# Layer 0 of a graph network stack on one core: two tiles a visit in place of three

## The chip, the core and the metric

The kernel runs on one core of a Trainium2 chip, in one launch. TensorE (PE in the profile) multiplies matrices into the eight banks of PSUM, VectorE (DVE), ScalarE (ACT) and GpSimd (POOL) work on vectors, and SP (SyncE) issues transfers. Each runs its own program in order, and they wait for one another through counting semaphores. The metric is the time of one execution in microseconds on the device.

## What is computed

Four layers over 2048 nodes with 64 features, each `x = x + layer(relu(layernorm(x)), adj)`. The change is in layer 0 alone, an attention with 8 heads and two kinds of edges (adj is 0 or 1):

```python
Q = h @ Qw + Qb; K = h @ Kw + Kb; V = h @ Vw + Vb
S1 = einsum('id,kdh->ikh', Q, A1); S2 = einsum('jd,kdh->jkh', K, A2)
e = S1[rows[:, None], kidx] + S2[rows[None, :], kidx]
e = leaky_relu(e, negative_slope=0.2)
attn = softmax(e, axis=1)
out = einsum('ijh,jhd->ihd', attn, Vh).reshape(n, h * d) @ Pw + Pb
```

The scores are rank-one sums, so exp(leaky_relu(s1 + s2)) can be built from products and maxima of exponentials of vectors, which is what the kernel does, with no exponential per element.

## The kernel before

**Tiles.** A tile is one head, 128 source nodes j and 512 target nodes i. There are 8 heads x 4 blocks of i x 16 tiles of j = 512 tiles (TILES0), numbered k, with j fastest. 16 tiles in a row share a block of i: a row block.

**One tile's way through the engines.** GpSimd writes the value for edges of kind 0 into one of 16 ring buffers in SBUF (line 368). TensorE crosses two vectors, held as three bf16 parts each, into the PSUM slot k mod 6 (`cross`, line 1053, 18 rows deep; in the profile "18*128"). ScalarE applies ReLU with scale -1 in place (line 851). TensorE adds a second product onto it, the floor (`raise_floor`, line 1061, "9*128"). VectorE copies the slot into the ring buffer where adj is 1 (`select`, copy_predicated, line 530). The finished tile is then read twice by TensorE: by `aggregate` (line 1074, fp32, two tiles at once, each in 64 columns of the array, into bank 6) and by `denominators` (line 1084, fp32, four tiles at once, each in 32 columns, into bank 7). An aggregate is 4 matmul records in the trace, a denominator 8. Per four tiles there are two aggregates and one denominator; one of these three is a "unit", and there are 384 units.

Tile k uses the 32 rows of the array from 32 (k mod 4) on, for its cross and its floor.

**The order on TensorE.** It is written out by hand as visits v. A visit issues the floors of the tiles that visit v - 1 crossed (`trio(v - 1)`), then the crosses of `trio(v)`, then the units from `units(v)` to `units(v + 1)`. The first unit comes in visit 3. A floor waits for its ReLU (`relus`), a cross for the select of the tile six before it, whose slot it takes (`selected`), an aggregate for the selects of its two tiles.

**The others.** ScalarE goes over the same visits: the ReLUs of `trio(v)`, and with the tenth and eleventh unit of every twelve the copies of bank 6 (line 839, `main_out`) and bank 7 (line 846, `den_out`) out of PSUM, at the end of a row block. VectorE selects tile by tile, with a small reciprocal (lines 537 and 538) and an addition (line 546) once per row block. GpSimd fills the ring in the order of the tiles and waits for a denominator before it writes over four old tiles; once per row block it also normalises (line 356). SP moves the denominators out and back and stages the next heads' vectors.

Of the kernel before, what the change touches and what calls it, by code (L numbers as in the profile page):

```python
# [42 lines left out]
def gnn_stack(nc, x_d, adj_d, Qw, Qb, Kw, Kb, Vw, Vb, a_rel, Pw, Pb, w_k, w_q, W2, a2, out_d):  # L43
# [14 lines left out]
    BLOCKS = N // HALF  # L58
    PER_HEAD = BLOCKS * NT
    SLOTS = 6  # L60
    TRIO = 3
    MAIN, DEN = 6, 7
    BLKS = 4
    NINE = PARTS * PARTS
# [4 lines left out]
    with ctx:  # L69
# [141 lines left out]
        BY_ROW = H * BLOCKS - 2  # L211
        VISITS = -(-TILES0 // TRIO)
        UNITS = TILES0 // 4 * 3

        def units(v):

            return min(max(9 * (v - 3) // 4, 0), UNITS)

        def trio(v):

            return range(TRIO * v, min(TRIO * v + TRIO, TILES0)) if 0 <= v < VISITS else ()

        LAST = next(v for v in range(2 * VISITS) if units(v) == UNITS)

        block = ctx.enter_context(nc.Block())
# [566 lines left out]
        def _(act):  # L792
# [55 lines left out]
            for v in range(LAST):  # L848
                for k in trio(v):
                    act.wait_ge(s["crossed"], k + 1)  # L850
                    act.activation(ps[:, k % SLOTS, :], ps[:, k % SLOTS, :], ACT.Relu, scale=-1.0).then_inc(s["relus"], 1)  # L851
                for u in range(units(v), units(v + 1)):
                    if u % 12 == 10:
                        main_out(u // 12)
                    if u % 12 == 11:
                        den_out(u // 12)
# [77 lines left out]
        def _(pe):  # L934
# [157 lines left out]
            for v in range(LAST):  # L1092
                for k in trio(v - 1):
                    raise_floor(k)
                for k in trio(v):
                    cross(k)
                for u in range(units(v), units(v + 1)):
                    if u % 3 < 2:
                        aggregate(4 * (u // 3) + 2 * (u % 3))
                    else:  # L1100
                        denominators(4 * (u // 3))
# [201 lines left out]
```

## Time and profile before

| | us |
|---|---|
| median of 3 runs | 1080.58 |
| lowest, highest | 1079.04, 1087.63 |
| the profiled execution | 1082.16 |
| its span | 1079.9 |
| layer 0's loop in it, first cross to last denominator | 92 to 574 |

| engine | busy us, share of the span |
|---|---|
| TensorE matmuls | 937.5, 87% |
| VectorE | 728.5, 67% |
| GpSimd | 555.8, 51% |
| ScalarE | 546.0, 51% |

The granted clock of TensorE is 0.888 of full in the mean over the span. The span is from the first to the last instruction that the profiler saw. In the timelines one row is a run of equal instructions: start and length in us, engine, line, operation, what it writes and reads with shapes, count, and in brackets how long the engine was idle before and what ended that. The length of a run reaches to the end of its last instruction, so runs of a pipelined engine overlap.

### The profile page before, as it was taken

How to read it: one execution, taken by the hardware profiler on the slowest of the kernel's cores; microseconds unless marked ns; L12 is line 12 of the kernel's file. 1: busy time of each engine (PE TensorE's matmuls, PEld its weight loads, DVE VectorE, ACT ScalarE, POOL GpSimd, SP SyncE). 2: the span in 40 equal slices, each digit the busy share in tenths (PEclk: the TensorE clock that was granted, in tenths of full speed). 3: DMA queues.
4: the chain of work that ended last, by engine and by line, in shares of the span. 5: the costliest groups of instructions: out<-in, count | busy, mean ns of one | idle time of the engine just before them, and what ended most of it. 6: DMA issues, size and time to landing. Idle time of an engine off the chain costs nothing.

```text
span 1079.9 us, 14479 instructions
## 1 busy us (share of the span) xinstructions
PE 937.5 (87%) x5239; PEld 336.0 (31%) x5239; DVE 728.5 (67%) x1145; ACT 546.0 (51%) x943; POOL 555.8 (51%) x658
## 2 busy tenths in 40 slices
PE   1996999999999999999996599999667939999970
PEld 1762222222222222222223522333262334555430
DVE  3145777777778777777774567411328667999987
ACT  0374666666665666656660076100100137899970
POOL 2006788898889888888870000000000007799962
PEclk8566999999999999999997579999857965999995
DMA  9472002021211121120000000000000000000000
GB/s 196 64 156 80 12 21 75 21 71 33 66 38 59 33 67 35 28 73 22 22 21 1 0 1 1 1 1 1 1 0 39 1 1 0 1 1 1 1 0 19
DMA packets 24940, 34.05 MB, mean 32 GB/s; under 512 B 16219, under 2 KB 16363, under 8 KB 23718
## 3 DMA queue, kind: packets, MB, share of 16 engines
q1 hardware_dynamic: 22566, 24.75, 7.9%
q0 software_dynamic: 2304, 8.39, 4.4%
q8 instruction: 41, 0.67, 0.3%
q14 instruction: 29, 0.24, 0.1%
HBM read 40.22 MB, written 1.30 MB: 38 GB/s over the span
## 4 chain that ended last, share of the span: by engine, by line
PE 72%; DVE 16%; issue 4%; DMA 3%; SPq 2%; ACT 1%; POOL 1%; DVEq 0%; ACTq 0%; POOLq 0%
PE ps L1074 22%; PE ps L1084 11%; PE ps L1181 8%; PE ps L1061 5%; DVE big L411 4%; PE ps L1053 4%; PE ps L1215 3%; PE ps L1155 3%; PE ps L1251 3%; DVE big L724 2%; DMA big<-in_L_gnn_Pw_dram 2%; DVE big L408 2%; PE ps L1145 2%; PE ps L938 1%; PE ps L1223 1%
## 5 line engine op out<-in xcount | busy, mean ns | idle before, releaser
L530 DVE COPY_PREDICATED big<-mask,ps 128x512 f32<-128x512 uint8 x512 | 338.2, 724 | 115.2 <-PE ps L1061 107.6
L368 POOL TENSOR_SCALAR big<-big 128x512 f32<-128x512 f32 x512 | 356.3, 713 | 72.5 <-PE ps L1084 72.2
L851 ACT ACTIVATE ps<-ps 128x512 f32<-128x512 f32 x512 | 266.8, 582 | 167.1 <-PE ps L1053 167.1
L1074 PE MATMUL ps<-big 128*64 128x512 f32 x1024 | 258.9, 613 | 0.0
L380 POOL TENSOR_TENSOR big<-big 128x512 f32<-128x512 f32 x40 | 67.3, 1684 | 342.1 <-ACT big L911 342.1
L1084 PE MATMUL ps<-big 128*32 128x512 f32 x1024 | 136.5, 605 | 0.0
L1053 PE MATMUL ps<-op_r,op_l 18*128 18x512 bf16 x512 | 110.3, 386 | 8.4 <-DMA op_r<-split_scratch 7.1
L1074 PEld LDWEIGHTS ps<-big 128*64 128x64 f32 x1024 | 58.6, 136 | 135.7 <-issue 98.4
L1251 PE MATMUL ps<-big 66*128 66x512 f32 x160 | 86.1, 668 | 2.2 <-DVE big L697 1.3
L411 DVE TENSOR_TENSOR big<-big,mask 128x512 f32<-128x512 f32 (+1 forms) x72 | 65.8, 933 | 12.8 <-ACT big L871 11.5
L1061 PE MATMUL ps<-op_r,op_l 9*128 9x512 bf16 x512 | 70.7, 390 | 2.0 <-ACT ps L851 2.0
L384 POOL TENSOR_TENSOR big<-big 128x512 f32<-128x512 f32 x40 | 63.6, 1590 | 6.7 <-ACT big L919 2.0
L617 DVE TENSOR_REDUCE work<-ps 128x256 f32<-128x512 f32 x16 | 11.1, 691 | 77.9 <-PE ps L1165 77.9
L1061 PEld LDWEIGHTS ps<-op_r,op_l 9*128 9x128 bf16 x512 | 17.2, 91 | 145.3 <-ACT ps L851 106.0
L1181 PE MATMUL ps<-big,y_nat 128*64 128x512 f32 x256 | 59.0, 609 | 1.9 <-DVE y_nat L407 1.9
L879 ACT ACTIVATE hT<-ps 128x512 f32<-128x512 f32 x16 | 9.2, 598 | 92.3 <-PE ps L1181 89.0
L938 PE MATMUL ps<-ident,h_nat 128*65 128x128 f32 (+1 forms) x64 | 13.9, 407 | 41.9 <-DVE h_nat L411 18.1
L1084 PEld LDWEIGHTS ps<-big 128*32 128x32 f32 x1024 | 20.1, 107 | 83.3 <-issue 83.3
L1267 PE MATMUL ps<-big,h_nat 128*66 128x512 f32 x80 | 43.0, 625 | 2.8 <-DVE big L411 2.8
L1251 PEld LDWEIGHTS ps<-big 66*128 66x128 f32 x160 | 30.9, 210 | 38.2 <-issue 18.2
L667 DVE SCALAR_TENSOR_TENSOR big<-big,mask 128x1024 f32<-128x1024 f32 x32 | 38.4, 1280 | 4.9 <-DMA big<-max_scratch 4.9
L871 ACT ACTIVATE big<-ps,small 128x1024 f32<-128x1024 f32 x32 | 34.0, 1111 | 13.4 <-PE ps L1145 13.2
(235 smaller groups left out, 1137.1 us busy)
## 6 DMA issues: line engine op xcount, KB each, us to landing
big<-max_scratch SPq DMA_DIRECT2D x9, 1024.0 KB, 4.9
big<-in_adj_dram POOLq DMA_DIRECT2D x16, 512.0 KB, 6.5
big<-rden_scratch SPq DMA_DIRECT2D x30, 256.0 KB, 3.3
op_l<-split_scratch SPq DMA_DIRECT2D x64, 36.0 KB
op_r<-split_scratch SPq DMA_DIRECT2D x64, 36.0 KB
x_nat<-in_x_dram SPq DMA_DIRECT2D x1, 512.0 KB, 4.1
out_dram<-x_nat SPq DMA_DIRECT2D x1, 512.0 KB, 3.8
den_scratch<-y_nat SPq DMA_DIRECT2D x30, 8.0 KB
```

The source lines that it names most:

```text
L368: pool.tensor_scalar(ring[:, k % RING, :], vrow[:, head % 2, i0:i0 + HALF], HUGE, g0[:, head, jt:jt + 1], ALU.min, ALU.max).then_inc(s["ba ...
L380: pool.tensor_tensor(wB[:, u, :], wB[:, u, :], wA[:, u, :], ALU.subtract).then_inc(s["ratio"], 1)
L384: pool.tensor_tensor(wD[:, u, :], wD[:, u, :], wC[:, u, :], ALU.subtract).then_inc(s["art"], 1)
L411: return dve.tensor_tensor(out, a, b, op)
L530: dve.copy_predicated(ring[:, k % RING, :], mask[:, jt, i0:i0 + HALF], ps[:, k % SLOTS, :])\
L851: act.activation(ps[:, k % SLOTS, :], ps[:, k % SLOTS, :], ACT.Relu, scale=-1.0).then_inc(s["relus"], 1)
L1053: pe.matmul(ps[:, k % SLOTS, :], op_l[g:g + 2 * NINE, head % 2, jt * P:(jt + 1) * P], op_r[g:g + 2 * NINE, head % 2, i0:i0 + HALF], start= ...
L1061: pe.matmul(ps[:, k % SLOTS, :], op_l[g:g + NINE, head % 2, jt * P:(jt + 1) * P], op_r[g:g + NINE, head % 2, i0:i0 + HALF], start=False, s ...
L1074: m = pe.matmul(ps[w * D:(w + 1) * D, MAIN, :], vp[:, head, jt + w, :], ring[:, (u + w) % RING, :], start=(jt == 0), stop=(jt == NT - 2))
L1084: m = pe.matmul(ps[32 * w:32 * (w + 1), DEN, :], q0[:, head, jt + w:jt + w + 1].to_broadcast([P, 32]), ring[:, (u + w) % RING, :], start=( ...
L1181: m = pe.matmul(ps[w * D:(w + 1) * D, 4 + c, :], Y[n - 1][:, jt, :], eT[:, jt, c * HALF:(c + 1) * HALF], start=(jp == 0), stop=(jp == NT / ...
L1251: pe.matmul(ps[:, bank, :], lhs3[0:DX, jt * P:(jt + 1) * P], rhs[0:DX, c * HALF:(c + 1) * HALF], start=True, stop=True).then_inc(sem, 1)
```

## The change

Two numbers of layer 0's order: a visit holds two tiles instead of three, and the units advance by 3/2 a visit instead of 9/4. Per tile that is 3/4 of a unit either way. The six PSUM slots stay as they are.

```diff
@@ -58,7 +58,7 @@
     SLOTS = 6
-    TRIO = 3
+    TRIO = 2
     MAIN, DEN = 6, 7
@@ -214,7 +214,7 @@
         def units(v):
 
-            return min(max(9 * (v - 3) // 4, 0), UNITS)
+            return min(max(3 * (v - 3) // 2, 0), UNITS)
```

TensorE's program at the start of the loop before (L1053 cross, L1061 floor, L1074 aggregate with two instructions of the program each, L1084 denominator with four):

```order
L1053 MATMUL ps<-op_r,op_l 128x512 x3
L1074 MATMUL ps<-big 64x512 x4
L1061 MATMUL ps<-op_r,op_l 128x512 x3
L1053 MATMUL ps<-op_r,op_l 128x512 x3
L1084 MATMUL ps<-big 32x512 x4
L1074 MATMUL ps<-big 64x512 x2
L1061 MATMUL ps<-op_r,op_l 128x512 x3
L1053 MATMUL ps<-op_r,op_l 128x512 x3
L1074 MATMUL ps<-big 64x512 x2
L1084 MATMUL ps<-big 32x512 x4
```

and the same place of the changed program:

```order
L1053 MATMUL ps<-op_r,op_l 128x512 x2
L1074 MATMUL ps<-big 64x512 x2
L1061 MATMUL ps<-op_r,op_l 128x512 x2
L1053 MATMUL ps<-op_r,op_l 128x512 x2
L1074 MATMUL ps<-big 64x512 x2
L1084 MATMUL ps<-big 32x512 x4
L1061 MATMUL ps<-op_r,op_l 128x512 x2
L1053 MATMUL ps<-op_r,op_l 128x512 x2
L1074 MATMUL ps<-big 64x512 x2
L1061 MATMUL ps<-op_r,op_l 128x512 x2
```

Between the crosses and the next floors there were always two or three units; now there is one aggregate, or an aggregate and a denominator, by turns, to the end of the loop.

ScalarE's program where row blocks end (L851 the ReLU, L839 and L846 the two copies), before:

```order
L839 ACTIVATE big<-ps 128x512
L851 ACTIVATE ps<-ps 128x512 x3
L846 ACTIVATE y_nat<-ps 128x512
L851 ACTIVATE ps<-ps 128x512 x15
L839 ACTIVATE big<-ps 128x512
L846 ACTIVATE y_nat<-ps 128x512
```

and in the changed program:

```order
L851 ACTIVATE ps<-ps 128x512 x16
L839 ACTIVATE big<-ps 128x512
L846 ACTIVATE y_nat<-ps 128x512
L851 ACTIVATE ps<-ps 128x512 x16
L839 ACTIVATE big<-ps 128x512
L846 ACTIVATE y_nat<-ps 128x512
```

The two copies now always follow the ReLUs of one and the same visit, where before ReLUs of a visit stood between them in one row block of three.

## Rows read from the trace of the kernel before

**Rows 1.** The page: busy shares, the chain by engine and line, costly groups.

```profile
PE 937.5 (87%) x5239; PEld 336.0 (31%) x5239; DVE 728.5 (67%) x1145; ACT 546.0 (51%) x943; POOL 555.8 (51%) x658
...
PE 72%; DVE 16%; issue 4%; DMA 3%; SPq 2%; ACT 1%; POOL 1%; DVEq 0%; ACTq 0%; POOLq 0%
PE ps L1074 22%; PE ps L1084 11%; PE ps L1181 8%; PE ps L1061 5%; DVE big L411 4%; PE ps L1053 4%; PE ps L1215 3%; PE ps L1155 3%; PE ps L1251 3%; DVE big L724 2%; DMA big<-in_L_gnn_Pw_dram 2%; DVE big L408 2%; PE ps L1145 2%; PE ps L938 1%; PE ps L1223 1%
...
L530 DVE COPY_PREDICATED big<-mask,ps 128x512 f32<-128x512 uint8 x512 | 338.2, 724 | 115.2 <-PE ps L1061 107.6
L368 POOL TENSOR_SCALAR big<-big 128x512 f32<-128x512 f32 x512 | 356.3, 713 | 72.5 <-PE ps L1084 72.2
```

**Rows 2.** Busy time by engine in one stretch, visits 5 to 171.

```profile
core 0: us, PE busy (x) PEld busy (x) DVE busy (x) ACT busy (x) POOL busy (x), PEclk, DMA share, GB/s
106.42:568.16 461.74, 460.43 (x2993) 100.31 (x2992) 356.81 (x585) 290.90 (x559) 392.57 (x531) 1.00 0.14 41
```

**Rows 3.** The chain that ended last, by time: start us, us, engine, line.

```profile
216.53 0.32 PE ps L1061 x3
216.85 0.21 PE ps L1053 x3
217.07 1.01 PE ps L1074 x4
218.07 0.99 PE ps L1084 x8
...
223.01 1.87 PE ps L1074 x8
...
227.42 0.32 PE ps L1061 x3
227.74 0.57 PE ps L1053 x3
```

**Rows 4.** Waits, weight loads only, 106 to 568 us: total us, times, longest.

```profile
PEld ps L1053 <- DVE big L530: 12.4, 32, 1.1
```

**Rows 5.** Timeline of TensorE, 224.80 to 224.90 us: start, us, line, tiles.

```profile
224.81 0.39 PE L1061 MATMUL ps<-op_r,op_l 9*128 9x512 bf16 x3
224.82 0.39 PE L1053 MATMUL ps<-op_r,op_l 18*128 18x512 bf16 x1
```

**Rows 6.** Timeline of all engines, the loop's last two visits with floors.

```profile
564.77 0.59 PE L1053 MATMUL ps<-op_r,op_l 18*128 18x512 bf16 x2
...
565.29 1.07 ACT L851 ACTIVATE ps<-ps 128x512 f32<-128x512 f32 x2 [0.98 <-PE ps L1053]
...
568.16 0.39 PE L1061 MATMUL ps<-op_r,op_l 9*128 9x512 bf16 x2
...
568.48 1.94 PE L1074 MATMUL ps<-big 128*64 128x512 f32 x8
```

**Rows 7.** Timeline of all engines, the loop's start: start, us, idle before.

```profile
97.45 1.56 ACT L851 ACTIVATE ps<-ps 128x512 f32<-128x512 f32 x3 [0.73 <-PE ps L1053]
...
98.08 1.58 PE L1061 MATMUL ps<-op_r,op_l 9*128 9x512 bf16 x3 [0.70 <-ACT ps L851]
...
99.07 0.61 PE L1053 MATMUL ps<-op_r,op_l 18*128 18x512 bf16 x3
...
99.61 3.68 PE L1074 MATMUL ps<-big 128*64 128x512 f32 x8
...
103.22 0.61 PE L1061 MATMUL ps<-op_r,op_l 9*128 9x512 bf16 x3
```

**Rows 8.** Timeline of all engines where a row block ends.

```profile
131.01 0.59 PE L1053 MATMUL ps<-op_r,op_l 18*128 18x512 bf16 x3
131.14 0.60 ACT L846 ACTIVATE y_nat<-ps 128x512 f32<-128x512 f32 x1
...
131.63 1.57 ACT L851 ACTIVATE ps<-ps 128x512 f32<-128x512 f32 x3
```

**Rows 9.** Busy time by engine in one stretch of layer 2, columns as rows 2.

```profile
821.00:869.00 48.00, 44.01 (x282) 14.99 (x278) 37.36 (x36) 5.93 (x10) 0.00 (x0) 0.99 0.00 1
```

## The prediction

> **What bounds the kernel now.** I read the page first. TensorE is busy 87% of the span and carries 72% of the chain that ended last; lines 1074 and 1084, the aggregates and denominators of layer 0, are the largest pieces of it [rows 1]. So I asked for the layer 0 loop alone, cut from the floors of visit 5 (106.42 us) to those of visit 171 (568.16 us). That is 166 visits of three tiles, 498 tiles in 461.74 us at full granted clock, 0.927 us a tile, and TensorE shows 460.43 us busy while VectorE shows 356.81, ScalarE 290.90, GpSimd 392.57 [rows 2]. The change touches only this loop, and every tile that gets dearer by 10 ns costs 5 us.
>
> A busy share of 99.7% does not say that nobody waits: a matmul's time in the trace covers its pipeline, so short stalls vanish in it. The chain of work in order of time is better. One pattern of four visits (12 tiles) runs from 216.53 to 227.42 us, 10.89 us, and its pieces are: floors of three tiles 0.32 us, then crosses 0.21, an aggregate alone 1.01, a denominator 0.99, two aggregates in a row 1.87 [rows 3]. Sum: 4 x 0.53 + 2 x 1.87 + 2 x 1.01 + 3 x 0.99 = 10.85. At that pace 498 tiles need 41.5 x 10.89 = 452 us; the missing 10 us are visits in which a cross stands for its slot, as the last piece shows (0.57 in place of 0.21) [rows 3]. The view of waits has them under line 1053 waiting for VectorE's select, 32 times [rows 4]. These waits are what two tiles a visit on six slots can remove.
>
> **The change, part by part.**
>
> *Matmuls.* Nothing is added or removed: 512 crosses, 512 floors, 256 aggregates, 128 denominators either way. Only the grouping moves. Per 12 tiles there were four visits; now there are six, alternately "floors 2, crosses 2, one aggregate" and "floors 2, crosses 2, one aggregate, one denominator".
>
> *Floors with crosses.* Tile k uses row strip 32 (k mod 4). With three tiles, the floors take three strips and only the first cross finds the fourth strip free: it starts 0.01 us after the floors, together with them [rows 5], and the other two wait for a strip, which is the 0.21 piece in the chain [rows 3]. With two tiles the floors and crosses of one visit are four tiles in a row, so four different strips, and all four can run together. Four at once is what rows 5 already show. The price is then that of one batch: in the last visit before, two floors with no cross behind them, the aggregate starts 568.48 - 568.16 = 0.32 us after the floors [rows 6]. So 6 x 0.32 = 1.92 replaces 4 x 0.53 = 2.12. From the other side, if the crosses did not join, it is 0.53 per visit (a rival below).
>
> *Aggregates.* No two aggregates stand in a row any more. Two pairs of 1.87 become four of 1.01: +0.30 per 12 tiles [rows 3]. TensorE's own work is then 1.92 + 6 x 1.01 + 3 x 0.99 = 10.95 per 12 tiles, against 10.85 of before by the same pieces: even, to 0.1 us. The Trainium skill, page "TensorEngine Tiling", Key Properties, says that a change of tiling mode drains TensorE, which speaks against smaller groups: here the runs of one kind rise from 11 to 15 per 12 tiles. The chain's pieces already hold that price (a lone aggregate is 0.07 dearer than half a pair), so the rule adds nothing to the sum.
>
> *Slots.* The second cross of visit v waits for the select of tile 2v - 5, whose floor was issued at the start of visit v - 2, so two whole visits (3.96 us together, below) lie between; before, it was the visit just ahead (2.4 to 3.4 us) for three selects of 0.72 us plus the odd row addition. I take the 10 us of waits as gone.
>
> *The ReLU between cross and floor.* This is the part that costs. TensorE runs in order, and visit v + 1 opens with the floors of the tiles that visit v crossed; each needs its ScalarE pass. In full-clock rows: from the crosses to the first ReLU 565.29 - 564.77 = 0.52 us; two ReLUs together 1.07 us [rows 6]; from the end of the last ReLU to the floor and the crosses behind it 99.07 - (97.45 + 1.56) = 0.06 at most, take 0.05 [rows 7]. Cross to second floor is 0.52 + 1.07 + 0.05 = 1.64 us and cannot be shorter. What covers it before: two or three units, so 0.53 + 1.87 = 2.40 at the least, against 0.52 + 1.56 + 0.05 = 2.13 for three ReLUs; hidden, with 0.27 to spare. After: a visit with an aggregate and a denominator is 0.32 + 1.01 + 0.99 = 2.32, hidden. A visit with one aggregate is 0.32 + 1.01 = 1.33, and the second floor is ready only at 1.64. TensorE stands 0.31 us, with the next two crosses queued behind that floor, and ScalarE starts its next two ReLUs later in turn, so nothing catches up. A visit got 1/3 shorter in TensorE's work, but the chain cross-ReLU-floor lost only one ReLU of 0.49.
>
> The Trainium skill, page "ScalarE: Activation LUTs", Rules for kernel authors, budgets about 0.3 us and 0.83 ns an element for an ACTIVATE, so 0.72 us for these by estimate; two would be 1.45, the one-aggregate visit 2.02, and the loss some 47 us larger. The trace does not agree: two in a row take 1.07 [rows 6], and the row decides.
>
> *Row blocks.* Once in 16 tiles ScalarE also copies the main and the denominator bank. In an existing visit of just the new kind (one aggregate, one denominator) the denominator's copy starts at 131.14 and the next ReLU at 131.63, where the cross at 131.01 alone would allow 131.53 [rows 8]: 0.10 us late. Before it was inside the 0.27 of slack. After, the visit that follows is a one-aggregate visit, where lateness counts: 31 x 0.10 = 3.1 us.
>
> *Other engines.* GpSimd fills ring slots released by denominators (0.71 us a tile) and VectorE selects at 0.72 [rows 1]; four tiles now take 3.96 us, more than either's 2.9, so both have more room. SP's row staging follows the blocks and gets more time too.
>
> *Start and end.* Visits 0 to 2 hold no unit, and each is shorter by one ReLU, -1.5 us; but more of the first units then fall before the clock rises (a pair of aggregates takes 3.61 us there, from 99.61 to 103.22, against 1.87 [rows 7]), which takes back some 0.7. After the last floors one unit fewer is left, with its share of waiting: -0.5. Together about -1.3.
>
> **Sum.** Four tiles: 1.64 + 2.32 = 3.96. 498 tiles: 124.5 x 3.96 = 493.0, + 3.1 = 496.1, against 461.7: +34.4. With start and end: +33. The profiled execution took 1082.2 us (span 1079.9), so 1115; the median of the timed runs is 1.6 lower, 1080.6, so I forecast 1114.
>
> **Rivals.**
> 1. *The ReLU is hidden after all, not slower* (7%). Then four tiles take TensorE's own 1.33 + 2.32 = 3.65, 498 tiles 454, the waits of the crosses are gone, and the kernel takes 1082 - 7 - 1 = 1074, for the timed median 1072. It needs the second floor to be ready 1.33 us after its cross: ReLU latency and work smaller by 0.31 of 1.64, that is the 0.52 of rows 6 nearly halved or the two ReLUs at 0.38 each. For it: rival 1 is what a count of busy time says, since ScalarE is busy only 63% of the loop. Against it: all three terms are rows, and they repeat at the start, where floors do follow ReLUs directly [rows 7].
> 2. *The crosses do not join the floors* (4%). Each visit then opens with 0.53; the cross comes 0.21 behind the second floor, so 1.85 + 2.53 = 4.38, 498 tiles 545 + 3, and the kernel takes 1168. For it: two crosses behind two floors are in no row. Against it: rows 5, with four strips at work.
> 3. *The clock falls in the gaps* (3%). TensorE would now stand 0.31 of 3.96 us, 8%. In a stretch of layer 2 with 3.99 us idle of 48 (8%) the granted clock read 0.99 [rows 9], that is the 2.4 GHz level nearly throughout. If a tenth of the loop fell to 1.2 GHz, where aggregates take 3.61 in place of 1.87, it would cost about 0.1 x 0.93 x 454 = 42 us more: 1156. The Trainium skill, page "TensorE: Matmul & The Clock Gate", A second HAM failure mode, describes a kernel whose clock oscillated on short idles between groups while it cycled PSUM; this row shows hardly any at the same idle share.
>
> **How the numbers follow.** Forecast mechanism 86%, rivals 7, 4, 3. A measurement of this kernel tells about 1% from no change, 10.8 us. The chain term is 1.64 with 0.03 either way (+-4 us), the 10 us of cross waits might remain in part (up to +5), and half of the block term might not show (-2); a partly hidden ReLU wait of 0.25 in place of 0.31 would give 1107. Range 1105 to 1126. Rival 1 lies at -0.8%, mostly "same": faster 0.03, same 0.05, slower 0.92.
>
> **What would show it.** Per four tiles, floor to floor: 1.64 and 2.32, by turns. Crosses starting within 0.02 us of the floors ahead of them, and the aggregate 0.32 after. In the waits, line 1061 idle behind line 851 in about 128 visits, as at the start, and line 1053 behind VectorE gone. ScalarE busy the same, about 291 us over a loop of 496. It is wrong if the one-aggregate visits last 1.33 (rival 1) or the aggregate comes 0.53 after the floors (rival 2), or the granted clock in 110 to 600 us is below 1.00 (rival 3).

## The result, and the profile after

The changed kernel takes 1113.7 us in the median of four runs (1110.5 to 1118.7), the kernel before 1079.8 beside it: a ratio of 1.0305, 95% interval 1.0236 to 1.0374. It is slower by 34 us. The profiled execution took 1111.3 us with a span of 1109.1.

| | before | after |
|---|---|---|
| up to layer 0's first cross | 92.3 us | 95.2 us |
| layer 0 loop, first cross to last denominator's start | 481.4 us | 516.5 us |
| four tiles, mean over the 498 tiles from tile 12 on | 3.71 us | 3.98 us |
| from there to the end | 506.2 us | 497.4 us |
| span | 1079.9 us | 1109.1 us |

The page of the kernel after, in the order of [rows 1]: busy shares, the chain by engine and line, and VectorE's select.

```profile
PE 967.6 (87%) x5239; PEld 337.8 (30%) x5239; DVE 740.4 (67%) x1145; ACT 553.3 (50%) x943; POOL 556.1 (50%) x658
...
PE 76%; DVE 15%; issue 4%; DMA 2%; ACT 2%; SPq 1%; DVEq 0%
PE ps L1074 23%; PE ps L1084 11%; PE ps L1061 11%; PE ps L1181 7%; DVE big L411 4%; PE ps L1215 3%; PE ps L1155 3%; PE ps L1251 2%; PE ps L1004 2%; PE ps L965 2%; DVE big L724 2%; DMA big<-in_L_gnn_Pw_dram 2%; DVE big L408 2%; PE ps L938 1%; PE ps L1145 1%
...
L530 DVE COPY_PREDICATED big<-mask,ps 128x512 f32<-128x512 uint8 x512 | 343.8, 726 | 135.0 <-PE ps L1061 132.8
```

The share of line 1061, the floors, in the chain doubled, from 5 to 11%, with as many floors as before. The select costs the same per instruction, 0.73 us, and VectorE only waits longer for the floors. The loop in the columns of [rows 2], cut from a pair of visits near its start to one near its end:

```profile
109.50:606.00 496.50, 495.00 (x2994) 105.23 (x2992) 367.39 (x584) 297.95 (x561) 391.57 (x529) 1.00 0.13 38
```

TensorE reads 99.7% busy again, at full clock again, in a stretch in which it stands 0.28 us of every 3.94. The busy share shows nothing of it. The chain in order of time does (start, length, what; compare [rows 3]):

```profile
202.61 0.32 PE ps L1061 x2
202.94 0.01 PE ps L1053 x2
202.94 1.01 PE ps L1074 x4
203.95 0.60 PE ps L1061 x2
204.55 0.01 PE ps L1053 x2
204.56 1.01 PE ps L1074 x4
205.56 0.99 PE ps L1084 x8
206.56 0.32 PE ps L1061 x2
```

The floors of one visit take 0.32 us and those of the next 0.60, by turns, and the crosses 0.01: they run with the floors, where before they added 0.21. From 202.61 to 206.56 is 3.95 us for four tiles. The same place in the timeline of all engines, whose starts are up to 0.07 us earlier than the chain's, says why the second pair of floors takes 0.60:

```profile
202.55 0.39 PE L1061 MATMUL ps<-op_r,op_l 9*128 9x512 bf16 x2
...
202.55 0.39 PE L1053 MATMUL ps<-op_r,op_l 18*128 18x512 bf16 x2
...
202.87 1.08 PE L1074 MATMUL ps<-big 128*64 128x512 f32 x4
203.04 1.07 ACT L851 ACTIVATE ps<-ps 128x512 f32<-128x512 f32 x2 [1.29 <-PE ps L1053]
...
203.88 0.67 PE L1061 MATMUL ps<-op_r,op_l 9*128 9x512 bf16 x2
204.16 0.09 PEld L1061 LDWEIGHTS ps<-op_r,op_l 9*128 9x128 bf16 x1 [0.19 <-ACT ps L851]
...
204.17 0.39 PE L1053 MATMUL ps<-op_r,op_l 18*128 18x512 bf16 x2
```

In this one-aggregate visit the crosses start at 202.55 together with the floors, the aggregate 0.32 us later at 202.87, the two ReLUs at 203.04. The next visit opens with its first floor at 203.88 as soon as the aggregate leaves room, second floor at 204.16 when the second ReLU (203.04 + 1.07 = 204.11) is done, crosses right behind. 204.16 - 202.55 = 1.61 us. The weight load of the second floor is idle until then, put down to ScalarE. In the waits between 100 and 600 us:

```profile
PEld ps L1061 <- ACT ps L851: 234.6, 373, 1.6
...
PEld ps L1053 <- DVE big L530: 0.6, 1, 0.6
```

The first row holds much idle time of weight loads that lies beside running matmuls, so its sum is no loss; the second is: one late cross in place of the 32 of [rows 4].

After the loop the changed kernel is 8.8 us quicker, in code that the change doesn't touch. The same columns, the rest of the program, after and then before:

```profile
612.20:1109.00 496.80, 386.96 (x1759) 179.64 (x1755) 331.69 (x489) 209.73 (x323) 138.02 (x83) 0.85 0.01 4
```

```profile
574.30:1079.90 505.60, 398.03 (x1755) 186.10 (x1755) 331.25 (x489) 209.94 (x323) 137.95 (x83) 0.83 0.01 4
```

The last column but two is the granted clock: 0.85 against 0.83. VectorE's busy time agrees within 0.5 us; TensorE's is 11 us less. Which stretches of the later layers run at 1.2 and which at 2.4 GHz differs between these two executions, and I put the 8.8 us down to it; no run varies it alone. The start of the loop is touched as well: up to the floor of tile 12 the kernel before took 14.2 us from its first cross here and 13.6 in the run e9_before_short_add below, with the same code up to there. From tile 12 on the loop runs at 1.00, so the experiments below are read by their loop and periods as well as by their time.

### The profile page after: what moved, and what is told of

It is laid out like the page before. It is cut to its first block, busy times and chain, and to the rows that moved or that the text cites. A ratio compares the mean times of both kernels' runs of the same rounds, so it can differ in the third digit from the quotient of the medians.

```text
span 1109.1 us, 14479 instructions
## 1 busy us (share of the span) xinstructions
PE 967.6 (87%) x5239; PEld 337.8 (30%) x5239; DVE 740.4 (67%) x1145; ACT 553.3 (50%) x943; POOL 556.1 (50%) x658
## 4 chain that ended last, share of the span: by engine, by line
PE 76%; DVE 15%; issue 4%; DMA 2%; ACT 2%; SPq 1%; DVEq 0%
PE ps L1074 23%; PE ps L1084 11%; PE ps L1061 11%; PE ps L1181 7%; DVE big L411 4%; PE ps L1215 3%; PE ps L1155 3%; PE ps L1251 2%; PE ps L1004 2%; PE ps L965 2%; DVE big L724 2%; DMA big<-in_L_gnn_Pw_dram 2%; DVE big L408 2%; PE ps L938 1%; PE ps L1145 1%
## 5 line engine op out<-in xcount | busy, mean ns | idle before, releaser
L530 DVE COPY_PREDICATED big<-mask,ps 128x512 f32<-128x512 uint8 x512 | 343.8, 726 | 135.0 <-PE ps L1061 132.8
L851 ACT ACTIVATE ps<-ps 128x512 f32<-128x512 f32 x512 | 274.4, 579 | 193.1 <-PE ps L1053 193.1
L1074 PE MATMUL ps<-big 128*64 128x512 f32 x1024 | 277.7, 621 | 0.0
L1061 PE MATMUL ps<-op_r,op_l 9*128 9x512 bf16 x512 | 139.3, 388 | 3.2 <-ACT ps L851 2.0
L1084 PE MATMUL ps<-big 128*32 128x512 f32 x1024 | 136.8, 606 | 0.0
L1061 PEld LDWEIGHTS ps<-op_r,op_l 9*128 9x128 bf16 x512 | 35.2, 90 | 242.8 <-ACT ps L851 241.4
L1053 PE MATMUL ps<-op_r,op_l 18*128 18x512 bf16 x512 | 100.8, 389 | 1.5 <-DVE mask L522 1.2
L1251 PE MATMUL ps<-big 66*128 66x512 f32 x160 | 81.4, 631 | 4.4 <-DVE big L724 2.2
L1074 PEld LDWEIGHTS ps<-big 128*64 128x64 f32 x1024 | 50.9, 135 | 59.4 <-issue 32.5
L1084 PEld LDWEIGHTS ps<-big 128*32 128x32 f32 x1024 | 20.1, 107 | 104.7 <-issue 104.7
L1251 PEld LDWEIGHTS ps<-big 66*128 66x128 f32 x160 | 28.5, 199 | 38.1 <-issue 15.2
## 6 DMA issues: line engine op xcount, KB each, us to landing
big<-in_adj_dram POOLq DMA_DIRECT2D x16, 512.0 KB, 8.3
x_nat<-in_x_dram SPq DMA_DIRECT2D x1, 512.0 KB, 4.2
out_dram<-x_nat SPq DMA_DIRECT2D x1, 512.0 KB, 3.8
```

Of the source, the lines that this page charges most:

```text
L530: dve.copy_predicated(ring[:, k % RING, :], mask[:, jt, i0:i0 + HALF], ps[:, k % SLOTS, :])\
L1053: pe.matmul(ps[:, k % SLOTS, :], op_l[g:g + 2 * NINE, head % 2, jt * P:(jt + 1) * P], op_r[g:g + 2 * NINE, head % 2, i0:i0 + HALF], start= ...
L1061: pe.matmul(ps[:, k % SLOTS, :], op_l[g:g + NINE, head % 2, jt * P:(jt + 1) * P], op_r[g:g + NINE, head % 2, i0:i0 + HALF], start=False, s ...
L1074: m = pe.matmul(ps[w * D:(w + 1) * D, MAIN, :], vp[:, head, jt + w, :], ring[:, (u + w) % RING, :], start=(jt == 0), stop=(jt == NT - 2))
L1084: m = pe.matmul(ps[32 * w:32 * (w + 1), DEN, :], q0[:, head, jt + w:jt + w + 1].to_broadcast([P, 32]), ring[:, (u + w) % RING, :], start=( ...
L1251: pe.matmul(ps[:, bank, :], lhs3[0:DX, jt * P:(jt + 1) * P], rhs[0:DX, c * HALF:(c + 1) * HALF], start=True, stop=True).then_inc(sem, 1)
```

## The experiments

All edits are to the changed kernel unless said. "Loop" is from the first cross to the last denominator's start in the profiled execution, and a period is the time from a floor to the floor four tiles later.

### Is it the ReLU? Half of each ReLU

```diff
-act.activation(ps[:, k % SLOTS, :], ps[:, k % SLOTS, :], ACT.Relu, scale=-1.0)
+act.activation(ps[:, k % SLOTS, 0:HALF // 2], ps[:, k % SLOTS, 0:HALF // 2], ACT.Relu, scale=-1.0)
```

> The changed kernel with the ReLU on 256 of each slot's 512 columns (the other half of the scores goes without it). Theory (TensorE waits for the second ReLU in each one-aggregate visit): cross to second floor falls from 1.61 to about 1.2 us, under the 1.33 us that the aggregate covers, so a pair of visits takes 1.34 + 2.33 = 3.67 us in place of 3.94, the 0.15 us at each row block goes too: -35 - 4, so 1073 to 1077 us. Rival (the loss is TensorE's own, in changing more often between kinds of matmul): nothing moves, 1113.

> The kernel before with the same cut, ReLU on half of each slot's columns. Theory: in its visits the ReLU has 0.27 us to spare, so nothing is gained, 1080 within 0.5%. Rival (ScalarE's work sets the pace in either kernel): 10 us or more are gained.

Measured: 1073.8 us (10 runs) for the changed kernel with the cut, loop 475.3 against 516.5; ratio to the kernel before 0.997 (0.992 to 1.002). For the kernel before with the cut 1080.7 us, ratio 1.002 (0.997 to 1.006), loop 479.1 against 481.4. The timeline of the cut changed kernel in a one-aggregate visit right behind a row block: crosses, the copy of bank 7, the two ReLUs, the next floors:

```profile
200.14 0.39 PE L1053 MATMUL ps<-op_r,op_l 18*128 18x512 bf16 x2
200.27 0.60 ACT L846 ACTIVATE y_nat<-ps 128x512 f32<-128x512 f32 x1 [0.42 <-PE ps L1084]
...
200.76 0.65 ACT L851 ACTIVATE ps<-ps 128x256 f32<-128x256 f32 x2
...
201.47 0.39 PE L1061 MATMUL ps<-op_r,op_l 9*128 9x512 bf16 x2
```

Even this one, with the ReLUs held back by the copy until 200.76, is over at 201.47, 1.33 us after its crosses, both floors at once. The period is 3.67 us everywhere but in one place, at a row block too. So the loss hangs on the length of the ReLU chain. With the ReLUs short in both kernels the finer cutting is no loss: the changed one's loop is the shorter by 3.8 us (475.3 against 479.1), since the joined crosses and the missing late ones outweigh what single aggregates cost. In the kernel before, where two or three units cover three ReLUs, the cut is worth 2.3 us of loop and nothing measurable in the whole. This also gives the price of the rival that I had put at 7%: it would have come out at 1072 to 1074.

### Do the crosses join because their strips are free?

```diff
-g = 32 * (k % 4)
+g = 32 * (k % 2)
```

in `cross` and `raise_floor`.

> The changed kernel with tile k on row strip 32 (k mod 2), so that two crosses find both strips taken by two floors. Theory (the crosses join the floors only because their strips are free): the crosses start 0.21 us after the floors; a pair takes 2.54 + 1.82 = 4.36 us in place of 3.94, 128 pairs: +54, 1167 us. Rival (the strips don't matter; the crosses are short anyway): within 10 us of 1114.

Measured: 1159.8 us, ratio 1.078 (1.066 to 1.089), period 4.305, loop 564.2. The chain:

```profile
303.62 0.32 PE ps L1061 x2
303.95 0.22 PE ps L1053 x2
304.16 1.01 PE ps L1074 x4
305.17 0.54 PE ps L1061 x2
305.71 0.22 PE ps L1053 x2
```

The crosses cost 0.22 again in every visit. It came 7 us under what was expected: I had priced a one-aggregate visit at 1.82 us, and it is 1.77. The strips' worth is (4.305 - 3.944) x 128 = 46 us: without four strips the change would have cost 80 us in place of 34.

### Were the late crosses of before worth 10 us, and did the slots' slack remove them?

```diff
-SLOTS = 6
+SLOTS = 4
```

> The changed kernel with four PSUM slots in place of six: a cross waits for a select whose floor came one visit before, not two. Theory (six slots at two tiles a visit took the cross waits away): the second cross after a one-aggregate visit waits until some 1.9 us after the floors, +0.28 us a pair and more where VectorE has a row block's extra work, 1145 to 1160 us, and line 1053 stands behind VectorE over 100 times. Rival (the slack in slots is worth nothing): 1114.

Measured: 1176.8 us, ratio 1.093 (1.083 to 1.104), loop 576.6. Slower than either expectation. Periods are 4.21; from tile 108 on, where VectorE's first row addition stands, one of four is 5.11. The chain where a row block's addition stands, and, from 304.96 on, an ordinary pair:

```profile
301.19 0.61 PE ps L1061 x2
301.80 0.73 DVE big L530
...
302.57 0.39 PE ps L1053
...
304.96 0.32 PE ps L1061 x2
305.28 0.01 PE ps L1053 x2
305.29 1.01 PE ps L1074 x4
306.30 0.60 PE ps L1061 x2
306.89 0.28 PE ps L1053 x2
```

The ordinary pair has the expected wait, 0.28 us between the second floor and the crosses. What I had priced too low is the other one: VectorE's row addition (line 546) sits between two selects, and with a visit less of slack its full 0.9 us appears in TensorE. There are 26 additions, one in each row block from the seventh on; the 25 periods of the loop's middle that hold one are 27 us longer together than as many of 4.21. The direction of the step holds: at two tiles a visit, six slots hide VectorE's unevenness but for one late cross, and four hide none of it.

The same addition in the kernel before, cut short:

```diff
-dve.tensor_tensor(accT[:, i0:i0 + HALF], accT[:, i0:i0 + HALF], blk[:, n % BLKS, :], ALU.add)
+dve.tensor_tensor(accT[:, i0:i0 + 32], accT[:, i0:i0 + 32], blk[:, n % BLKS, 0:32], ALU.add)
```

> The kernel before with the row block's addition on 32 of 512 columns (the rest of the sum over heads is left out). Theory (the late crosses of before come from this addition of 0.9 us ahead of a select): the waits of line 1053 behind VectorE mostly go, 6 to 9 us off the layer 0 loop of 481 us. Rival (they come from the reciprocals or from the selects themselves): the loop stays within 2 us. The whole kernel's time is no measure here, the later layers vary by more.

Measured, one execution: loop 475.9 against 481.4, of which 0.6 lies ahead of tile 12, where the programs are equal. Of line 1053's waits in the same stretch as [rows 4]:

```profile
PEld ps L1053 <- DVE big L530: 6.0, 15, 0.7
```

12.4 us in 32 times became 6.0 in 15. The addition made about half of the late crosses, 4.9 us from tile 12 on, less than expected; cut short, it still takes 0.34 us in place of 0.85. Most of what remains, 10 of 15, is the cross of a tile 16 n + 6, which waits for the first select behind VectorE's reciprocal pair (lines 537, 538). That is a reading of their places in the timeline; no run takes this half away by itself.

### The row block

```diff
-                    if u % 12 == 11:
-                        den_out(u // 12)
+                    if u % 12 == 0 and u:
+                        den_out(u // 12 - 1)
+            den_out(UNITS // 12 - 1)
```

> The changed kernel with ScalarE's copy of bank 7 put behind the ReLUs of the next, one-aggregate visit instead of ahead of them. Theory (the copy makes the next ReLUs 0.15 us late, in a visit that has no cover): the four-tile period at a row block falls from 4.09 to 3.94 us, the loop of 516.5 us gets 31 x 0.15 = 4.6 us shorter. Rival (what is late there comes from elsewhere, as the denominators' bank): the period stays at 4.09.

The timeline of the changed kernel at a row block, before this edit:

```profile
198.47 0.39 PE L1053 MATMUL ps<-op_r,op_l 18*128 18x512 bf16 x2
198.59 0.60 ACT L846 ACTIVATE y_nat<-ps 128x512 f32<-128x512 f32 x1 [0.42 <-PE ps L1084]
...
199.09 1.08 ACT L851 ACTIVATE ps<-ps 128x512 f32<-128x512 f32 x2
...
199.79 0.81 PE L1061 MATMUL ps<-op_r,op_l 9*128 9x512 bf16 x2
...
200.22 0.39 PE L1053 MATMUL ps<-op_r,op_l 18*128 18x512 bf16 x2
```

The copy of bank 7 starts at 198.59, 0.12 us after the crosses, and the ReLUs follow at 199.09 where 0.49 us after the crosses, 198.96, was due. The second floor and the next crosses stand at 200.22, 1.75 us after the crosses in place of 1.61: 0.14 late. With the copy moved, the 30 periods of 4.09 are 3.94 or 3.95, and the loop is 512.0 us: 4.5 shorter, as expected. This is one execution, so its 1109.7 us for the whole are not used.

### The order of the units

```diff
-return min(max(3 * (v - 3) // 2, 0), UNITS)
+return min(max((3 * (v - 3) + 1) // 2, 0), UNITS)
```

> The changed kernel with the units rounded up instead of down: two aggregates in one visit, the denominator alone in the next. TensorE's work per pair is 0.32 + 1.87 and 0.32 + 1.0. Theory (the one-unit visit stays at ReLU's 1.61, the two aggregates in a row save 0.14): 2.19 + 1.61 = 3.80 us a pair in place of 3.94, -18: 1095 us. Rival (the order of units makes no difference): 1113.

Measured: 1094.2 us, ratio 1.013 (1.009 to 1.017), period 3.807, loop 497.8. Two aggregates in a row save 0.14 us where the pieces of [rows 3] give 0.15, and the lone denominator's visit is as long as the lone aggregate's, 1.61 us, since the ReLU sets it.

### Floors two visits behind their crosses

```diff
-                for k in trio(v - 1):
+                for k in trio(v - 2):
                     raise_floor(k)
```

with `units` one visit later.

> The changed kernel with each floor issued two visits after its cross instead of one. Theory: the ReLU is hidden, but the slot's select is now late: its floor comes one visit before the cross that takes the slot, ready some 1.9 us after the floors, so a cross after a one-aggregate visit waits 0.57 us and a pair takes 4.2 us: 1145 us. Rival (only the ReLU's chain matters): 1075.

Measured: 1180.2 us, ratio 1.091 (1.085 to 1.097); periods 4.21 and once per row block 5.11. The pair takes the expected 4.2 us, but the whole is 35 us above what was expected, and the row additions, which the expectation had left out, are 27 of it. The ReLU is hidden, both groups of floors take 0.32 us in the chain, and the slots have become the bound: this is the four-slot kernel over again, row addition included. It isn't as clean a test as it was meant to be. Its chain at a row addition and, from 305.41 on, the floors and crosses of a visit and the crosses of the next one:

```profile
301.37 0.86 DVE big L546
...
302.25 0.73 DVE big L530
...
305.41 0.32 PE ps L1061 x2
305.73 0.22 PE ps L1053 x2
...
307.28 0.35 PE ps L1053 x2
```

Visits v - 2 and v cross tiles that are four apart, so on the same two strips, and the crosses don't join the floors: they add 0.22 us in one visit and 0.35 in the next. The very last cross waits for a select: in the timeline it starts at 307.24, 1.90 us after the floors of the visit before (305.34), as the expectation has it. So the 0.22 of the visit before lies inside that wait and the pair stays at 4.2. This run shows that the slots bind here, and nothing about the strips.

### Three and one

Cover and ReLUs can be matched instead: cross three tiles ahead of two units, one tile ahead of one.

```diff
 def units(v):
-    return min(max(3 * (v - 3) // 2, 0), UNITS)
+    return min(max(3 * (v - 4) // 2, 0), UNITS)
...
 def trio(v):
-    return range(TRIO * v, min(TRIO * v + TRIO, TILES0)) if 0 <= v < VISITS else ()
+    return range(4 * (v // 2) + v % 2, 4 * (v // 2) + (4 if v % 2 else 1)) if 0 <= v < VISITS else ()
```

> Tiles in groups of three and one by turns in place of two and two: the visit with an aggregate and a denominator crosses three tiles, the visit with one aggregate crosses one. Floors and crosses of a visit are still four tiles on four strips. Theory: three ReLUs need 2.11 of 2.33 us, one ReLU 1.12 of 1.33, both hidden, 3.67 us for four tiles: 1073 to 1078 us. Rival (three crosses for slots released by selects one short visit back wait for VectorE): 0.2 us or more a pair, 1098 or more.

and with `(3 * (v - 5) + 1) // 2` in place of `3 * (v - 4) // 2`, so that the two aggregates stand together and the denominator alone:

> Groups of three and one with two aggregates in the visit that crosses three tiles and the denominator alone in the other. Theory: 2.19 us for the three (ReLU needs 2.11) and 1.33 for the one, 3.52 us for four tiles against 3.63 and waits of before: 1056 to 1062 us, faster than the kernel before by about 2%. Rival (with 0.08 us of slack the ReLU or VectorE's select is late each time): 1075 or more.

Measured: 1078.7 us (12 runs), ratio 0.996 (0.992 to 0.999), period 3.67, a little above the range expected; and 1059.9 us (6 runs), ratio 0.980 (0.974 to 0.985), period 3.516, 3.56 once a row block, loop 461.7. The first is within 1% of the kernel before, the second is 2% faster than it and 5% faster than the changed one. Chain and late crosses of the second:

```profile
306.07 0.32 PE ps L1061
306.39 0.01 PE ps L1053 x3
306.40 1.87 PE ps L1074 x8
308.26 0.32 PE ps L1061 x3
308.59 0.00 PE ps L1053
308.59 0.99 PE ps L1084 x8
```

```profile
PEld ps L1053 <- DVE big L530: 0.5, 1, 0.5
```

Every floor group is 0.32, every cross group at most 0.01, one cross is late in the whole stretch: what is left is TensorE's own work, 0.32 + 1.87 + 0.32 + 0.99.

## Why the prediction was right

- **Matmuls: the crosses join the floors.** Right: 0.01 in the chain, the aggregate 0.32 after. With two strips the 0.21 came back.
- **Aggregates one by one.** Right in size: 0.14 us for each pair broken up, where 0.15 was written, shown by putting them together again (3.944 to 3.807).
- **Slots.** Right: the late crosses fell from 32 to one. What they had cost in the kernel before is less sharply known than the 10 us that I wrote: the row addition made 4.9 us of it; the rest was not taken away by a run.
- **The ReLU.** Right, within 0.03 us: 1.61 us from cross to second floor against 1.64 written, the first ReLU starting 0.49 us after the crosses where I had 0.52. With half the ReLU the loss was gone. Two signs were written too simply: line 1061 stands behind line 851 in 373 rows of the view and not 128, since it counts weight loads of the long visits and of first floors too, and ScalarE is busy 298 us of the loop, not 291, since runs of two ReLUs take 0.53 us a tile and runs of three 0.52.
- **Row blocks.** The mechanism right, the term too small: 0.10 us for each of 31 blocks was written; the period is 0.15 longer in 30 of them, 4.5 us in the loop against 3.1. Not in the forecast were eight longer periods, seven of 4.04 us where a head changes and one of 4.37, 1.1 us together. The pair at 3.944 in place of 3.96 gives back 2.0, so that the 498 tiles took 495.8 us against 496.1 written is partly small errors that offset one another.
- **Start and end.** The one term that was wrong, by 2.3 us. It was written as -1.3; the loop grew by 35 us, of which the 498 tiles in the middle are 34.1 (495.8 against 461.7, written 34.4), so start and end are +1.0. Up to the floor of tile 12 the changed kernel needs 15.7 us from its first cross, the one before 14.2 (13.6 in e9_before_short_add, so some tenths of this are chance). By then it has issued six units where the other had issued four, for it starts them after six tiles instead of nine. I had counted that the visits without units are shorter and not that two more units are done by the same tile, which by the counts explains it, though no run changed the start by itself; from the last floors to the end gives back 0.6 for one of them.
- **The clock.** 1.00 from 109.5 us to the loop's end with these gaps in it. The rest of the program was 8.8 us shorter in the profiled execution, at a higher granted clock, which the forecast had not spoken of: it wrote 1115 for this execution, which took 1111.3. That the median of four runs, which spread over 8 us, came out at 1113.7 against 1114 written is luck to that last digit; the loop's 35 us against 33 are the better measure of the forecast.
- **The ScalarE budget.** The budget that the Trainium skill, page "ScalarE: Activation LUTs", Rules for kernel authors, gives for an ACTIVATE would have made the loss some 47 us larger by estimate, and the row decided rightly: two ReLUs take 1.07 us here too. The budget is stated for an ACTIVATE with a pointer operand for its bias, and line 851 reads nothing but PSUM in the trace, so it was not a price for these ReLUs.

## What to carry to other kernels

Where an in-order engine hands tiles to another and takes them back a visit later, the cover of a visit must be longer than a fixed latency plus so much per tile; smaller visits shrink only the second part, and the thinnest visit decides, not the mean. Here that was 1.61 us for two tiles against 1.33 us of cover. So size the batch of each visit by the work behind it (three tiles ahead of two units, one ahead of one) rather than evenly, and keep equal work together where a switch of shape costs. Read the chain of work in order of time for this: the busy share stood at 99.7% in a loop with 7% of waiting in it.

## What the runs showed of the hardware

- Four matmuls of 9 or 18 rows on four different row strips, floors adding onto banks already written and crosses starting new ones, run together: an aggregate follows 0.32 us after the first of them, for two or for four of them alike ([rows 6] and the timeline of after). With two strips it is 0.54.
- Two ReLUs in a row on 256 columns of PSUM take 0.65 us, on 512 columns 1.07: half the columns take 61% of the time, so some 0.23 us of the pair doesn't go with the columns.
- How long the later layers run at the 1.2 GHz level differs between executions of programs that are equal there: 0.83 and 0.85 of full clock in the mean over 500 us, with 11 us of TensorE's busy time and 8.8 us of the span beside it.
